# Two-part one-pass products for all plain f32 products of an attention stage, and products with values in two groups of eight heads instead of four of four

## What is computed

```python
q = (layernorm(x) @ wq.T)          # 16 heads of 16, scaled by 1/16 with the scores
k, v = ctx @ wk.T, ctx @ wv.T
attn = softmax(q k^T / 16)         # per head, 256 x 256
x1 = x + tanh(g) * (merge(attn @ v) @ wo.T)
x2 = x1 + tanh(g_ffn) * L0_ffn(layernorm(x1))
D  = sqrt(max(aa + bb - 2 * a @ b.T, 0))   # a, b: context and layernorm(x2), 256 x 256 per batch entry
```

## Time and profile before

| | us |
|---|---|
| median of 3 runs | 1828.75 (1828.48 to 1829.92) |
| the profiled execution's own time | 1828.01 |
| its span, first to last instruction | 1826.2 |
| TensorE busy | 1414.0 (77%) |
| VectorE busy | 1420.9 (78%) |
| ScalarE busy | 1107.6 (61%) |
| GpSimd busy | 551.6 (30%) |

### The profile page before, as it was taken

How to read it: one execution, slowest core, us unless ns; L and a number is a source line. 1 busy time by engine, 2 the same in 40 slices (tenths; PEclk the granted TensorE clock), 3 DMA queues, 4 the chain that set the end, 5 groups by cost and what they waited for, 6 DMA issues and landing times. The chain is left out here.

```text
span 1826.2 us, 35776 instructions
## 1 busy us (share of the span) xinstructions
PE 1414.0 (77%) x10821; PEld 1072.6 (59%) x10821; DVE 1420.9 (78%) x4062; ACT 1107.6 (61%) x2395; POOL 551.6 (30%) x998
## 2 busy tenths in 40 slices
PE   5899999999999999999999986133332004899896
PEld 4578788888887888878888765000001002566664
DVE  6677777777777777777777642899998998999996
ACT  3476676676766767667677662243335002999997
POOL 3122222322222223222233221200000002778785
PEclk8899999999999999999999997555555555999999
DMA  5444445444444444444543310322220002222321
GB/s 175 139 129 116 138 125 146 121 116 140 124 135 124 117 142 130 118 129 123 147 123 107 111 42 18 99 59 61 60 45 11 0 0 81 76 87 92 100 76 47
DMA packets 322936, 179.49 MB, mean 98 GB/s; under 512 B 93793, under 2 KB 318193, under 8 KB 322802
## 3 DMA queue, kind: packets, MB, share of 16 engines
q1 hardware_dynamic: 322802, 178.07, 35.0%
HBM read 122.91 MB, written 50.33 MB: 95 GB/s over the span
## 5 line engine op out<-in xcount | busy, mean ns | idle before, releaser
L982 DVE TENSOR_REDUCE nmax<-s 128x2 f32<-128x512 f32 x512 | 327.0, 681 | 7.9 <-PE s L454 6.9
L709 ACT ACTIVATE pt<-s 128x512 f32<-128x512 f32 x512 | 281.0, 611 | 70.0 <-PE s L471 69.9
L1074 POOL TENSOR_TENSOR r<-rl 128x512 f32<-128x512 f32 x128 | 133.1, 1040 | 328.4 <-ACT rl L739 285.6
L454 PE MATMUL s<-kst,qst 96*128 96x256 bf16 x1024 | 158.2, 275 | 11.6 <-DVE nmax L982 8.0
L471 PE MATMUL s<-qst,kst 128*128 128x256 bf16 x1024 | 156.9, 275 | 1.1 <-ACT pt L709 0.8
L1341 PE MATMUL gate<-diag,one 128*128 128x512 f16 x35 | 21.3, 608 | 171.7 <-DVE left L1432 171.7
L739 ACT ACTIVATE rl<-wb,fscl 128x256 f32<-128x256 f32 x256 | 107.8, 476 | 64.7 <-PE wb L555 64.7
L551 PE MATMUL wb<-x2l,wfcT 128*128 128x256 f32 x512 | 143.3, 302 | 0.7 <-ACT dd L761 0.7
L485 PE MATMUL oacc<-pt,vw 128*32 128x256 f32 x2048 | 137.0, 385 | 6.4 <-ACT pt L709 6.0
L951 DVE TENSOR_TENSOR r2l<-r,r2h 128x512 fp32r<-128x512 f32 x128 | 88.6, 692 | 65.2 <-POOL r L1074 40.3
L418 PE MATMUL wb<-wprT,r2l 128*128 128x256 f32 x512 | 131.8, 296 | 6.9 <-DVE r2l L951 6.9
(11 more groups left out here) (270 smaller groups left out, 3951.9 us busy)
## 6 DMA issues: line engine op xcount, KB each, us to landing
kst<-k_parts_dram SPq DMA_DIRECT2D x384, 64.0 KB, 2.5
qst<-q_parts_dram SPq DMA_DIRECT2D x384, 64.0 KB, 2.4
k_parts_dram<-kp SPq DMA_DIRECT2D x32, 384.0 KB, 5.2
q_parts_dram<-qp SPq DMA_DIRECT2D x32, 384.0 KB, 3.1
xin<-in_x_dram SPq DMA_DIRECT2D x32, 256.0 KB, 2.8
cT<-in_ctx_T_dram SPq DMA_DIRECT2D x32, 256.0 KB, 2.7
xres<-in_x_dram SPq DMA_DIRECT2D x32, 256.0 KB, 3.1
cin<-in_ctx_dram SPq DMA_DIRECT2D x32, 256.0 KB, 4.6
```

What stands on the lines that cost most here:

```text
L454: last = pe.matmul(s1[h % 2][:, t, :], qst[b.p][0:MAXROW, h, t * P:t * P + P], kst[b.p][0:MAXROW, h, :], start=True, stop=True)
L709: act.activation(pt[h % (2 * HPG)][:], s2[h % 2][:], ACT.Exp).then_inc(e["expd"], 1)
L982: v.tensor_reduce(nmax[:, T * h:T * h + T], s1[h % 2][:], AX.X, ALU.max, negate=True)\
L1074: pool.tensor_tensor(r2[:], rl[:, k % 2], rl[:, k % 2], ALU.mult)\
```

## The change

- The five kinds of plain f32 products become sums of three F32R products, high x low, low x high and high x high (new function `three`). Every operand is held in two tiles: its F32R rounding, made by ScalarE, and the remainder, a subtraction.
- The remainders of the turned tiles are made by VectorE from PSUM: `x_low(a)` is its first step in an iteration, `on_low(z)` comes after maxima 2 and 3, `y_low(y)` after `ln1(nx)`.
- The context arrives in one raw tile each, `cT_raw` and `cD_raw`, no longer doubly buffered. ScalarE rounds it (`products_high(z)` after exponentials 0 to 3, `ctx_high(ct)` after the copy of the first half of heads), GpSimd subtracts (`products_low(z)` between the third part of the keys and `rstd`, `ctx_low(ct)` after the third part of the queries). SP's load of `cT` waits for the subtraction of the batch before and no longer for `v_mm`.
- `values` runs twice a batch with eight heads, at the places of the former groups 1 and 3, and fills both halves of `oacc`. `copy_half` copies 512 columns at once. Exponentials wait for the half of the heads that used the buffer.
- The split of the four weights is made once at the start. The raw weights lie in tiles that are used later, and so do `wfc`, `wpr` and `sclb`. SP's and GpSimd's semaphore increments after each wait go.

The diff, cut to its core:

```diff
-        xhat, xT = sb("xhat", [P, T, D]), sb("xT", [P, C, S])
-        cT = [sb(f"cT{p}", [P, C, S]) for p in range(2)]
-        cD = [sb(f"cD{p}", [P, C, S]) for p in range(2)]
+        xhat, xT = sb("xhat", [P, T, D]), [sb(f"xT{part}", [P, C, S], F32R) for part in "hl"]
+        cT = [[sb(f"cT{part}{p}", [P, C, S], F32R) for part in "hl"] for p in range(2)]
+        cT_raw, cD_raw = sb("cT_raw", [P, C, S]), sb("cD_raw", [P, C, S])
+        cD = [[sb(f"cD{part}{p}", [P, C, S], F32R) for part in "hl"] for p in range(2)]
...
-                w("v_mm", b.n - 1)
-                sp.dma_start(cT[b.p][:], ct_d[b.n].rearrange(feat, p=P)).then_inc(cT_in[b.p], 16)
+                w("c_low", b.n)
+                sp.dma_start(cT_raw[:], ct_d[b.n].rearrange(feat, p=P)).then_inc(e["cT_in"], 16)
 
             def load_ctx_products(b):
-                w("ab_mm", b.n - 1)
-                sp.dma_start(cD[b.p][:], ct_d[b.n].rearrange(feat, p=P)).then_inc(cD_in[b.p], 16)
+                w("d_low", b.n)
+                sp.dma_start(cD_raw[:], ct_d[b.n].rearrange(feat, p=P)).then_inc(e["cD_in"], 16)
...
-            def project(bank, wt, src, s):
+            def three(bank, lhs, rhs, c, block):
+                pe.matmul(bank, lhs[0][:, c, block], rhs[1][:, c, :], start=(c == 0), stop=False)
+                pe.matmul(bank, lhs[1][:, c, block], rhs[0][:, c, :], start=False, stop=False)
+                return pe.matmul(bank, lhs[0][:, c, block], rhs[0][:, c, :], start=False, stop=(c == C - 1))
+
+            def project(bank, lhs, rhs, s):
                 for m in range(C):
                     for c in range(C):
-                        last = pe.matmul(bank[:, m, :], wt[:, c, m * P:m * P + P], src[:, c, :],
-                                         start=(c == 0), stop=(c == C - 1))
+                        last = three(bank[:, m, :], lhs, rhs, c, slice(m * P, m * P + P))
                 last.then_inc(e[s], 1)
...
-                w("max_split", b.n - 1), w("xT_cp", b.n)
+                w("max_split", b.n - 1), w("x_low", b.n)
...
-                    w("xT_cp", b.n + 5), w("max_split", b.n + 3)
+                    w("x_low", b.n + 5), w("max_split", b.n + 3)
...
-            def values(b, g):
-
-                w("expd", NH * b.n + HPG * (g + 1), NH * NB)
-                if g == 0:
+            def values(b, half):
+                w("expd", NH * b.n + NH // 2 * (half + 1), NH * NB)
+                if half == 0:
                     if at(b, 0):
                         pe.wait_ge(e["w_made"], GPR_MADE)
                     w("vw_cp", b.n + 1)
-                w("o_cp", NG * b.n + g, NG * NB)
-                for t in range(T):
-                    for j in range(HPG):
-                        last = pe.matmul(oacc[HW * j:HW * j + HW, g % 2, :], vw[b.p][:, t, HPG * g + j, :],
-                                         pt[(HPG * g + j) % (2 * HPG)][:, t, :],
-                                         start=(t == 0), stop=(t == T - 1))
+                w("o_cp", 2 * b.n + half, 2 * NB)
+                for g in range(2):
+                    for t in range(T):
+                        for j in range(HPG):
+                            last = pe.matmul(oacc[HW * j:HW * j + HW, g, :], vw[b.p][:, t, NH // 2 * half + HPG * g + j, :],
+                                             pt[HPG * g + j][:, t, :], start=(t == 0), stop=(t == T - 1))
                 last.then_inc(e["av_mm"], 1)
...
-                w("yT_cp", b.n + 1), w(cD_in[b.p], 16 * (b.half + 1), 16 * NB)
+                w("y_low", b.n + 1), w("d_low", b.n + 1)
...
                     queries(a)
                 if there(i):
-                    values(i, 0)
                     scores2(i, 4, 6)
...
                     turn_xh2(z)
                 if there(i):
-                    values(i, 1)
+                    values(i, 0)
...
-                    values(i, 2)
                     scores2(i, 14, 16)
                 if there(s):
                     scores1(s, 14, 16)
                 if there(z):
                     fc(z, 2)
                 if there(i):
-                    values(i, 3)
+                    values(i, 1)
...
+            def weights_high():
+                act.wait_ge(e["w_straight"], 64)
+                for n, (high, low) in (("wk", wkT), ("wq", wqT), ("wv", wvT), ("wo", woT)):
+                    act.activation(high[:], straight[n], ACT.Copy).then_inc(e["w_act"], 1)
...
+            def ctx_high(b):
+                w("cT_in", 16 * (b.n + 1), 16 * NB)
+                w("v_mm", b.n - 1)
+                act.activation(cT[b.p][0][:], cT_raw[:], ACT.Copy).then_inc(e["c_high"], 1)
+
+            def products_high(b):
+                w("cD_in", 16 * (b.n + 1), 16 * NB)
+                w("ab_mm", b.n - 1)
+                act.activation(cD[b.p][0][:], cD_raw[:], ACT.Copy).then_inc(e["d_high"], 1)
...
-                    w("av_mm", NG * b.n + h // HPG - 1, NG * NB)
-                    act.activation(pt[h % (2 * HPG)][:], s2[h % 2][:], ACT.Exp).then_inc(e["expd"], 1)
-
-            def copy_group(b, g):
-                w("av_mm", NG * b.n + g + 1, NG * NB)
-                w("o_t", 2 * (b.n - 1) + g // 2 + 1, 2 * NB)
-                act.activation(osb[:, g, :], oacc[:, g % 2, :], ACT.Copy).then_inc(e["o_cp"], 1)
+                    w("av_mm", 2 * b.n + h // (NH // 2), 2 * NB)
+                    act.activation(pt[h % (2 * HPG)], s2[h % 2][:], ACT.Exp).then_inc(e["expd"], 1)
+
+            def copy_half(b, half):
+                w("av_mm", 2 * b.n + half + 1, 2 * NB)
+                w("o_t", 2 * (b.n - 1) + half + 1, 2 * NB)
+                act.activation(osb[:, 2 * half:2 * half + 2, :], oacc[:], ACT.Copy).then_inc(e["o_cp"], 1)
...
                     exps(i, 0, 4)
+                if there(z):
+                    products_high(z)
...
+                    copy_half(i, 0)
+                if there(ct):
+                    ctx_high(ct)
...
+            def weights_straight():
+                for k, (n, (high, low)) in enumerate((("wk", wkT), ("wq", wqT), ("wv", wvT), ("wo", woT))):
+                    v.wait_ge(e["w_act"], STRAIGHT_HIGH + k + 1)
+                    v.tensor_tensor(low[:], straight[n], high[:], ALU.subtract).then_inc(e["w_made"], 1)
...
+            def x_low(b):
+                w("xT_cp", b.n + 1)
+                v.tensor_tensor(xT[1][:], B_TURN_X[:], xT[0][:], ALU.subtract).then_inc(e["x_low"], 1)
+
+            def on_low(b):
+                w("onT_cp", b.n + 1)
+                v.tensor_tensor(onT[1][:], B_TURN_ON[:], onT[0][:], ALU.subtract).then_inc(e["on_low"], 1)
+
+            def y_low(b):
+                w("yT_cp", b.n + 1)
+                v.tensor_tensor(yT[1][:], B_TURN_Y[:], yT[0][:], ALU.subtract).then_inc(e["y_low"], 1)
...
                 if there(a):
+                    x_low(a)
                     k_remainder(a)
...
                     maxima(s, 2, 4)
+                if there(z):
+                    on_low(z)
...
                     ln1(nx)
+                if there(y):
+                    y_low(y)
...
+            def ctx_low(b):
+                w("c_high", b.n + 1)
+                high, low = cT[b.p]
+                pool.tensor_tensor(low[:], cT_raw[:], high[:], ALU.subtract).then_inc(e["c_low"], 1)
+
+            def products_low(b):
+                w("d_high", b.n + 1)
+                high, low = cD[b.p]
+                pool.tensor_tensor(low[:], cD_raw[:], high[:], ALU.subtract).then_inc(e["d_low"], 1)
...
                     parts(a, "k_parts", kr, kp)
+                if there(z):
+                    products_low(z)
                 rstd(i)
                 if there(y):
                     halves(y)
                 if there(a):
                     parts(a, "q_parts", qr, qp)
+                if there(ct):
+                    ctx_low(ct)
```

More of the change, by code:

```diff
@@ L66, in off, with done @@
         return Batch(self.half + k // 2, k % 2)
-def done(eng, sem, count, most, tick=None):
+def done(eng, sem, count, most):
     if isinstance(count, int):
@@ L78, in done @@
     eng.wait_ge(sem, count)
-    if tick is not None:
-        eng.sem_inc(tick, 1)
 class Chain:
@@ L115, in sem @@
             return ctx.enter_context(nc.semaphore(name))
-        wqT, wkT, wvT, woT = (sb(n, [P, C, D]) for n in ("wqT", "wkT", "wvT", "woT"))
+        wqT, wkT, wvT, woT = ([sb(n + part, [P, C, D], F32R) for part in "hl"] for n in ("wqT", "wkT", "wvT", "woT"))
         wfcT, fscl = sb("wfcT", [P, C, F], F32R), sb("fscl", [P, FT])
@@ L138, in attention_phase @@
         nsp = sb("nsp", [2 * NH, 2, P], BF16)
-        pt = [sb(f"pt{r}", [P, T, S]) for r in range(2 * HPG)]
+        pts = sb("pts", [P, 2 * HPG, T, S])
+        pt = [pts[:, r] for r in range(2 * HPG)]
         osb = sb("osb", [P, NG, S])
-        rs, on, onT = sb("rs", [P, T, NH // 2]), sb("on", [P, T, D]), sb("onT", [P, C, S])
+        rs, on = sb("rs", [P, T, NH // 2]), sb("on", [P, T, D])
```

(39 more changed lines are left out.)

67 lines of the change are left out of this document (35 added, 32 removed).

## The result

| | median us | against the kernel before |
|---|---|---|
| before | 1828.62 | 1 |
| after | 1922.32 (1917.64 to 1924.75) | 1.051 (95% interval 1.0488 to 1.0532) |

The change costs 94 us, nearly twice the 51 that were forecast (1880, range 1855 to 1898). The profiled execution took 1917.64 us, its span is 1915.4 us, 89.2 more than before. The last distances are written at 1229.9 instead of 1141.1, 88.8 later, so everything lies in the attention stage. There the first GpSimd power of a batch with all parts in it comes at 130.46 instead of 122.89: 7.6 us are lost at the start, the rest in the batches.

The account below looks back on a forecast made before the run. TensorE's instructions bound the attention stage (99.4% busy); after the change, waits would. 16.4 + 5.51 + 12.57 = 34.5 us a batch against 32.79, +51 over thirty batches, start about +2 less 1: 1828.01 becomes 1880, range 1855 to 1898.

Parts of the forecast that it names:

- a pause before the turned y: In each attention batch TensorE idles about 2 us before `turn_y`, until `yn` is done.
- one before scores 14 and 15: TensorE idles about 1 us before second scores 14 and 15, until the exponential is done.
- the power held by GpSimd itself: GpSimd's subtraction of the distances' context, before `rstd`, moves `rstd` and `turn_y` by 0.5 us.
- 16.4 to the turned y: From batch start to `turn_y`: 16.4 us, where it was 16.36.
- 12.57 to the next batch: From the second scores of head 8 to the next batch: 12.57 us, before 11.63.
- rival (5): TensorE's clock drops: a fifth of the batch at 1.2 in place of 2.4 GHz, 2000 us; chance 0.02.
- The start: Four weights rounded and subtracted before the first keys: about +2 us, less some 1 from cheaper products.
- 1.70 us a batch: TensorE's saving on products: keys 0.42; output projection, queries, values projection and distance products 0.32 each.
- rival (3): TensorE's work remains the bound in the attention stage: 1762 us, or 1795 with half the saving; chance 0.07.
- The chain to `yn`: From residual2 to `yn`, 7.87 us back to back without TensorE work after `proj(y, 1)`; TensorE had 0.4 in hand.
- Rival (1): The distances' context does not hold up `rstd`: +1.2 us a batch, 1865 us; chance 0.24.
- Theory B: Follow-up theory: the two-part products' roundings and subtractions on other engines cost the time; most of 94 us stays with four groups.

Follow-up runs that it names:

- e3: Changed kernel with 26 idle products of 128 columns in TensorE's pause before the turned y, nothing else: 1895.43 us, ratio 1.0369.
- e4: Changed kernel with the distances' context rounded behind `ctx_high` on ScalarE and subtracted behind `ctx_low` on GpSimd: 1874.17 us, ratio 1.0250.
- e6: Changed kernel with four value groups, distances' context steps out of the way of `rstd`, maxima 4 and 5 behind the query remainder: 1807.69 us, ratio 0.9889.
- e9: Changed kernel with only GpSimd's subtraction of the distances' context moved behind `rstd`: 1870.71 us, ratio 1.0233.
- e1: Changed kernel with the values back in four groups of four heads at their old places, two-part products kept: 1849.16 us, ratio 1.0115.
- e5: Changed kernel with values in four groups and the distances' context rounding and subtraction out of the way of `rstd`: 1817.91 us, ratio 0.9930.
- e10: Changed kernel, values in halves, distances' context steps out of the way and maxima 4 and 5 behind the query remainder: 1858.42 us, ratio 1.0163.
- e8: Changed kernel, values in halves, with only the maxima of heads 4 and 5 moved behind the query remainder: 1921.35 us.

## Why the prediction was wrong, point by point

**The sign and the mechanism held.** TensorE 92% busy and not faster, a pause before the turned y, one before scores 14 and 15, the power held by GpSimd itself: all are in the profile. The batch at full clock was forecast piece by piece: 16.4 to the turned y (421.31 - 404.72 = 16.59), 5.51 from there to second scores 8 (463.39 - 457.89 = 5.50 in the batch that kept its clock), 12.57 to the next batch (12.51, 428.44 to 440.95), in all 34.5 (34.60). Halves of 1.88 took 1.87.

**The step that failed is the clock**, rival (5): chance 0.02, with the sentence that a stretch of the last layer at 90% busy had kept 1.00. A busy share over 100 us says nothing of how the idle time is distributed. In that stretch of the last layer it is spread thin, and no pause is longer than 0.41 us; here 1.7 us of it lie in one piece. The Trainium skill, "TensorE: Matmul & The Clock Gate", What's actually happening, has activity release a throttle that is the default, and sets the clock by how busy TensorE has been recently; by that rule a piece of idle time counts where it lies. The trace agrees: 1.00 in the pause, 0.90 in the 1.7 us behind it, then 0.50. I cited the rule and let an average overrule it. The price was off too, the other way: I let 6 us of work take 12 in each batch (30 times 6 on 1880 is 2060, and not the 2000 that I wrote). A batch in which the clock fell took 1.7 us more (36.5 against 34.8), that is nine of 22, 0.7 us a batch in the mean, and by e3 27 us. The rival was written as a certain loss or none. It is one that strikes some batches, and no run shows which of several equal pauses it strikes.

**Two terms of the sum were too small.** From e3, without the clock's part, 1895 is left against 1880. The start costs 7.6 and was put at 1. The splitting of the weights and of the first context is not what was mis-sized: GpSimd's second power comes at 17.46 instead of 16.14, 1.3 later, and the fourth at 62.10 instead of 61.53. The time is lost from there to the first full batch, where the context's subtraction stands in front of the power for the first time:

```profile
93.91 1.27 POOL L1124 TENSOR_TENSOR cDl<-cD_raw,cDh 128x512 fp32r<-128x512 f32 x1 [9.48 <-ACT cDh L696]
95.14 1.01 POOL L1141 TENSOR_TENSOR ln_y<-ln_v,ln_pow 128x4 f32<-128x4 f32 x1
```

The kernel before is at this power at 91.08, and e4, with both steps of that context moved, at 89.07 and at the first full one at 121.20, earlier than the 122.89 before. How the 7.6 divide between the rounding, the subtraction and the clock in this stretch stays open. A batch is 34.8 in the mean and was put at 34.5: the subtraction took 1.27 in place of 1.16 and the power started at +14.44 instead of +14.15. The landing of the load scatters (3.6 to 5.2 us); that this makes the other batches longer is likely and not shown.

**What TensorE saves was too large.** 1.70 us a batch were forecast for the products. In e6, where TensorE is 98.9% busy, the batch is 0.82 shorter. From x to the turned y 0.92 are saved where 1.38 were counted (416.13 - 400.69 = 15.44 against 16.36): output projection to queries takes 1.52 and not 1.41, since the first F32R product of a run takes some 0.09 longer, and the keys start 0.65 behind x, held by fc's last relu. Behind that the turned halves wait 0.26 for the remainder of y. So the 1762 of rival (3) is out of reach of what the change saves: the fastest order tried, e6, with TensorE as the bound and the groups kept, takes 1808. The chain to `yn` was also said to hold no TensorE work after the second half of proj; it holds the output projection, which `residual1` reads. That did not bind: VectorE begins `residual1` at 515.48 without a wait.

**Rival (1)**, the context not in the way, had 1865; e9 measured it at 1871. **Theory B** is out as the whole cause by e1: the products alone cost 21 us and, with the context's rounding and subtraction moved (e5), save 10.

**The ledger of the 94 us**: the clock 27 (e3), the subtraction in front of the power without it 25 (e3 less e9), and 42 for the rest (e9 less the kernel before): the halves, 51 by e10 less e6, and 5 at the start (e9's first full power comes at 128.05), less what the products save. The last split isn't additive, since each wait covers part of the next.

## What to carry to other kernels

When an engine that is 99% busy gets less to do, look for the first chain on other engines that ran in parallel with the removed work: here the removal was worth no more than the slack of that chain, and a step added to it, on an engine that was 33% busy, was paid for. Work that stands in front of a wait may be what hides it, so the little switching saved by merging can cost the whole wait; and of TensorE ask not only how much it idles but whether the idle time lies in one piece, because a pause can cost the clock of the work behind it.

## What the hardware showed that I had not expected

The granted clock fell to 0.50 after a pause of 1.7 us in batches in which TensorE was otherwise busy nearly throughout, in nine of 22 batches and not in the others with the same pause. It did not fall in e4 with pauses of 1.49, but once in e1 behind 1.30, and in e8 behind pauses of 1.25 to 2.28 at another place. The length of one pause thus does not settle it, and what else does is not shown. Twenty-six idle products in the pause keep it at 1.00 and make the kernel 27 us faster. A GpSimd subtraction of 128 x 512 took 1.27 us with an F32R output, 1.16 with a bf16 output and its squares in f32 1.04; the inputs differ as well (the squares read one tile twice), so how much of it is the output's type is not shown.
